# Feed-forward pipeline in another order: the next x is turned in the transposition banks, the row is scaled and clipped by halves between the gate products

## The reference, cut to what matters

```python
def act_quant(x):                       # per token
    scale = 128 / clip(max(abs(x), axis=-1), 1e-5)
    return clip(round(x * scale), -128, 127) / scale
def bitlinear(x, w):   return einsum('bsh,oh->bso', act_quant(x), weight_quant(w))
def h_bitlinear(x, w): return einsum('bsh,oh->bso', act_quant(fwht(x)), weight_quant(w))
gate = bitlinear(x, w_gate)             # 512 -> 2048
up = bitlinear(x, w_up)                 # 512 -> 2048
return h_bitlinear(silu(gate) * up, w_down)   # Hadamard transform of 2048, 2048 -> 512
```

## Time and profile before

| | us |
|---|---|
| median of 3 runs | 2934.85 |
| lowest, highest | 2922.32, 2937.47 |
| the profiled execution | 2938.83 |
| its span in the trace | 2937.1 |
| TensorE products busy | 2063.3 (70%) |
| VectorE busy | 1879.4 (64%) |
| ScalarE busy | 1172.5 (40%) |
| GpSimd busy | 781.1 (27%) |

### The profile page before, as it was taken

How to read it: one execution, slowest core, us unless ns; L and a number is a source line. 1 busy time by engine, 2 the same in 40 slices (tenths; PEclk the granted TensorE clock), 3 DMA queues, 4 the chain that set the end, 5 groups by cost and what they waited for, 6 DMA issues and landing times. The chain is left out here.

```text
span 2937.1 us, 34386 instructions
## 1 busy us (share of the span) xinstructions
PE 2063.3 (70%) x12308; PEld 1395.3 (48%) x12308; DVE 1879.4 (64%) x3042; ACT 1172.5 (40%) x2024; POOL 781.1 (27%) x616
## 2 busy tenths in 40 slices
PE   5999994667777837877749999973002778777760
PEld 5777773222222214444437777751001667555550
DVE  3555664567777746877844566556887343688876
ACT  2323321475655623444422332224882212455640
POOL 1112122015958111111011112220000040466654
PEclk8999997598999869999978999987555589999995
DMA  4333232562524020000032332310000200699965
GB/s 136 95 66 66 45 65 80 147 179 82 153 76 135 18 90 1 1 1 1 1 93 58 66 66 44 66 23 16 0 0 0 103 1 0 234 309 305 307 224 165
DMA packets 83672, 258.06 MB, mean 88 GB/s; under 512 B 17312, under 2 KB 18848, under 8 KB 73424
## 3 DMA queue, kind: packets, MB, share of 16 engines
q0 software_dynamic: 29856, 153.33, 17.4%
q1 hardware_dynamic: 52656, 102.62, 12.7%
q10 hardware_dynamic: 1024, 0.26, 0.0%
HBM read 167.51 MB, written 37.79 MB: 70 GB/s over the span
## 5 line engine op out<-in xcount | busy, mean ns | idle before, releaser
L875 DVE TENSOR_REDUCE x_negm<-x_M 128x2 f32<-128x1024 f32 x256 | 309.3, 1223 | 115.2 <-PE x_M L935 114.8
L824 ACT ACTIVATE x_PT<-x_T 128x512 f32<-128x512 f32 x512 | 280.0, 598 | 202.7 <-PE x_T L955 197.8
L317 ACT ACTIVATE L_attn_PT<-L_attn_T 128x512 f32<-128x512 f32 x320 | 175.5, 595 | 361.1 <-PE L_attn_T L519 361.1
L387 DVE TENSOR_REDUCE L_attn_negm<-L_attn_M 128x2 f32<-128x1024 f32 (+1 forms) x192 | 191.9, 1040 | 58.1 <-PE L_attn_M L500 57.7
L224 POOL DMA_DIRECT2D L_attn_QKS<-L_attn_HL x64 | 34.8, 544 | 597.5 <-ACT L_attn_HL L302 563.7
L955 PE MATMUL x_T<-x_QS,x_KS 49*128 49x512 f32 x512 | 141.2, 548 | 65.6 <-ACT x_PT L824 43.9
L517 PE MATMUL L_attn_T<-L_attn_QKS 97*128 97x256 f32 (+3 forms) x512 | 165.7, 385 | 11.1 <-DMA L_attn_QKS<-L_attn_mT 9.0
L1381 PE MATMUL graph_P<-ident,graph_L 128*128 128x128 f32 x64 | 15.7, 427 | 214.3 <-DVE graph_L L1454 209.0
L964 PE MATMUL x_O<-x_PT,x_V 128*32 128x512 f32 x1024 | 155.7, 684 | 8.2 <-issue 8.2
L1402 ACT ACTIVATE graph_seen_a<-graph_SIM,graph_mid 128x512 bf16<-128x512 f32 x200 | 141.4, 709 | 34.5 <-DVE graph_mid L1434 34.5
L955 PEld LDWEIGHTS x_T<-x_QS,x_KS 49*128 49x128 f32 x512 | 52.1, 200 | 215.8 <-ACT x_PT L824 134.2
(11 more groups left out here) (370 smaller groups left out, 5642.7 us busy)
## 6 DMA issues: line engine op xcount, KB each, us to landing
L_attn_QKS<-L_attn_HL SPq DMA_DIRECT2D x192, 128.0 KB, 4.7
L_attn_QKS<-L_attn_HL POOLq DMA_DIRECT2D x192, 128.0 KB, 4.1
moe_y_rows<-slots_YS SPq DMA_DIRECT2D x48, 256.0 KB, 7.5
x_WRAW<-in_w_gateT POOLq DMA_DIRECT2D x8, 1024.0 KB, 7.3
x_QS<-x_xh SPq DMA_DIRECT2D x128, 64.0 KB, 2.4
x_WRAW<-in_w_upT POOLq DMA_DIRECT2D x8, 1024.0 KB, 5.4
x_WRAW<-in_w_downT POOLq DMA_DIRECT2D x8, 1024.0 KB, 6.2
ffn_w<-x_WTER POOLq DMA_DIRECT2D x12, 512.0 KB, 3.3
```

Source lines behind the costliest of these rows:

```text
L317: ac.activation(PT[:, s, bank], T[:, bank], ACT.Exp, scale=SCALE).then_inc(t_free, 1)
L387: last = ve.tensor_reduce(negm[:, g % 2, h0:h0 + nh, i], src, AX.X, ALU.max, negate=True)
L824: ac.activation(PT[:, s // 4, head(s), :], T[(STEPS_S * g + s) % 3][:], ACT.Exp, scale=SCALE).then_inc(t_free, 1)
L875: ve.tensor_reduce(negm[:, g % 2, u // 4:4:2, u % 4], m[:].rearrange("p (r k) -> p r k", r=2), AX.X, ALU.max, negate=True).then_inc(m_free, 1)
```

## The change

The same instructions are issued in another order, and two buffers change place or size. The next x is turned in the first bank of TT instead of the up bank of GU, between the projection and the second half of the transform, and XQT has two buffers. VectorE copies it behind X. The row's scale (ScalarE) and clip (VectorE) go to the next step, by halves, ahead of silu and INT of its first two quarters. The copies of R are split in the same way, and one butterfly stands ahead of the second split, three behind the second INT. The maximum of the row and its small instructions go behind X and the copy of XQT. The second of the 1024-wide operations goes behind the third INT. The turn of the first half of a row waits for the first two quarters of its tile only, and for the copy of the x that was turned in TT.

```diff
-        XQT = sb("XQT", [P, KC, P], BF16)
+        XQT = sb("XQT", [P, 2, KC, P], BF16)
...
+            def scale(t, v):
+                act.wait_ge(quant, QSTEPS * (t + 1))
+                ac.activation(Y[:, HALVES[v]], Y[:, HALVES[v]], ACT.Identity, scale=yscale[:, 0:1],
+                              bias=magic[:, 0:1]).then_inc(rounded, 1)
...
+            def clip(t, v):
+                if v == 0:
+                    dve.wait_ge(yt_full, 2 * t)
+                dve.wait_ge(rounded, 2 * t + v + 1)
+                ve.tensor_scalar(YQ[:, HALVES[v]], Y[:, HALVES[v]], MAGIC, QB - 1, ALU.subtract, ALU.min).then_inc(yq_done, 1)
...
                 if quantised(s):
                     dve.wait_ge(xt_full, s + 2)
-                    ve.tensor_copy(XQT[:].rearrange("p k n -> p (k n)"),
-                                   GU[:, BANK:BANK + 256].bitcast(BF16)).then_inc(xqt_made, 1)
+                    ve.tensor_copy(XQT[:, (s + 1) % 2].rearrange("p k n -> p (k n)"),
+                                   TT[:, 0:256].bitcast(BF16)).then_inc(xqt_made, 1)
...
             def turn_half(t, v):
                 if v == 0:
-                    if t >= 3:
+                    eng.wait_ge(xqt_made, min(t + 2, NTILE))
+                    if t + 1 >= NTILE:
                         eng.wait_ge(yt_free, 2 * (t - 2))
+                    eng.wait_ge(gu_free, 4 * t + 2)
+                else:
                     eng.wait_ge(gu_free, 4 * t + 4)
-                else:
                     eng.wait_ge(th_free, 2 * t + 1)
...
             def turn_x(t):
-                eng.wait_ge(gu_free, 4 * t)
+                if t >= 4:
+                    eng.wait_ge(yt_free, 2 * (t - 3))
+                elif t >= 2:
+                    eng.wait_ge(th_free, 2 * (t - 1))
                 eng.wait_ge(xq_done, t + 1)
```

More of the change, by code:

```diff
@@ L1136, in gate_up, with butterfly @@
                                         in1=SG[:, u % 2, :], op0=ALU.mult, op1=ALU.mult).then_inc(gu_free, 1)
[L1138 to L1145, removed]
+            def butterfly(t, n):
+                i, j = n // 2, n % 2
+                dve.wait_ge(h_copied, 2 * t + i + 1)
+                inst = ve.tensor_tensor(Y4[:, BANK * n:BANK * (n + 1)], R[i][:, 0:BANK], S13[:, BANK * i:BANK * (i + 1)],
+                                        (ALU.add, ALU.subtract)[j])
+                if n == 3:
+                    inst.then_inc(bf_done, 1)
+            def clip(t, v):
[3 more added lines that the diff above has]
+                ve.tensor_scalar(YQ[:, HALVES[v]], Y[:, HALVES[v]], MAGIC, QB - 1, ALU.subtract, ALU.min).then_inc(yq_done, 1)
             def step(s):
@@ L1151, in step @@
                     lower(s - 1, 0)
+                if projected(s):
+                    clip(s - 3, 0)
                 if gated(s):
@@ L1154, in step @@
                 if scaled(s):
-                    butterfly(s - 2)
+                    butterfly(s - 2, 0)
                 if transformed(s):
                     lower(s - 1, 1)
+                if projected(s):
+                    clip(s - 3, 1)
                 if gated(s):
@@ L1160, in step @@
                 if scaled(s):
+                    for n in range(1, 4):
+                        butterfly(s - 2, n)
+                    dve.wait_ge(bf_done, s - 1)
                     q(ve.tensor_tensor(Y2[:, 0:1024], Y4[:, 0:1024], Y4[:, 1024:], ALU.add))
-                    q(ve.tensor_tensor(Y2[:, 1024:], Y4[:, 0:1024], Y4[:, 1024:], ALU.subtract))
                 if gated(s):
@@ L1170, in step @@
                     q(ve.tensor_tensor(pairs(Y, 1), pairs(Y2, 0), pairs(Y2, 1), ALU.subtract))
+                if projected(s):
+                    t = s - 3
+                    dve.wait_ge(d_full, t + 1)
+                    ve.scalar_tensor_tensor(out=XF[:, t, :], in0=GU[:, 0:BANK], scalar=deq[:, t:t + 1],
+                                            in1=XF[:, t, :], op0=ALU.mult, op1=ALU.add).then_inc(d_free, 1)
+                if quantised(s):
+                    dve.wait_ge(xt_full, s + 2)
+                    ve.tensor_copy(XQT[:, (s + 1) % 2].rearrange("p k n -> p (k n)"),
+                                   TT[:, 0:256].bitcast(BF16)).then_inc(xqt_made, 1)
+                if scaled(s):
+                    t = s - 2
                     q(ve.tensor_reduce(ymax[:], Y, AX.X, ALU.max, apply_absolute_value=True))
@@ L1236, in gate_up @@
                     for k in range(KC):
-                        last = pe.matmul(GU[:, BANK * w:BANK * (w + 1)], XQT[:, k, :], W[:, k, BANK * u:BANK * (u + 1)],
+                        last = pe.matmul(GU[:, BANK * w:BANK * (w + 1)], XQT[:, t % 2, k, :], W[:, k, BANK * u:BANK * (u + 1)],
                                          start=(k == 0), stop=(k == KC - 1))
```

46 lines of the change are left out of this document (17 added, 29 removed).

## The result

| | us |
|---|---|
| changed kernel, median of 4 runs | 2897.34 (2893.98 to 2905.51) |
| before, median of 4 runs | 2936.16 (2922.32 to 2938.59) |
| ratio of the runs | 0.9869, 95% interval 0.9844 to 0.9894 |
| the profiled execution after | 2895.50, span 2893.8 |

What follows compares the result with a forecast made beforehand. A ring of exposed hand-offs between TensorE, ScalarE and VectorE bounds the feed-forward step. Gains 38.9 + 5.4 + 4.8 + 1, less 3 in the drain, make 47.1 us; forecast 2889 us, range 2873 to 2912.

Steps and rivals of the forecast that it cites:

- The ring: Feed-forward step's closed chain of hand-offs between TensorE, ScalarE and VectorE: 19.75 us a step, against 22.84 before.
- The arms beside it: Work parallel to the hand-off chain in a feed-forward step: each fits with 0 to 0.4 us of slack.
- The small waits: VectorE's steady step: pieces of 0.1 to 0.4 us ahead of INT0, INT1, the second split and X.
- step 3: Third feed-forward step: gains 5.4 us from 25.14, or 2 less if the clock stays low.
- the drain: Feed-forward stage's end after INT3 of step 15, 41.2 us before: a loss of 3 us (0 to 5).
- INT3 to INT0: From VectorE's instruction consuming the fourth gate product to the next step's first: 3.47 us instead of 5.00.
- INT1 to INT3: From VectorE's second gate-product instruction to its fourth, through transforms, projection and turn of x: terms adding to 12.81 us.
- The clock rival: Steady feed-forward steps: one fall of TensorE's clock in each, 13 x 1.4 = 18 us less gain, 2907 to 2914; chance 0.06.
- The near-tied arms: Feed-forward step: work parallel to the hand-offs late by 0.4 us at two places, 20.5 a step, 2900; chance 0.17.
- VectorE's floor: Feed-forward step: hand-offs shrink and VectorE's own 18.5 us bound it, 16 us more gain, 2873; chance 0.06.
- No effect: Feed-forward step: the projection wait moves ahead of the row maximum and eats the gain, 2935; chance 0.05.
- slower: Feed-forward step: TensorE stays at 1.2 GHz; at half of the steps 36 us slower, 2971; chance 0.04.

Runs made afterwards that it cites:

- rest_alone: Changed kernel with the turn of x put back in the up bank behind G3, one XQT buffer; step 21.16 us, ratio to the kernel before 0.9913.
- late_quarters: drain_max_first with two of the second transform's four groups moved into the pauses around the next step's G0; step 19.53 us, ratio to the kernel before 0.9839.
- late_again: late_quarters run a second time, beside the changed kernel on the same chip; step 19.53 us, ratio to the kernel before 0.9852.
- max_before_x: Changed kernel with the row maximum and its small instructions back ahead of X; step 21.90 us, ratio to the kernel before 0.9924.
- drain_max_first: Changed kernel with the row maximum ahead of X only in steps without gate products; drain 42.2 us, ratio to the kernel before 0.9853.
- stats_twice: Changed kernel with the statistics of x taken a second time behind INT3 on VectorE (0.60 us more); step 20.07 us, one run.
- pool_sub: late_quarters with the 1024-wide subtraction moved from VectorE to GpSimd; step 20.02 us, ratio to the kernel before 0.9876.

## Why the prediction was right

**The ring.** All seven terms came out within 0.2 us, the sum 1.3% off. The arms beside it stood close to where they were put. INT1 to X is 8.38, against 8.2 for VectorE's work and 8.25 for the end of the projection. The waits for silus are 0.24 to 0.51, forecast as 0.1 to 0.4. The small waits that were forecast ahead of the second split and of X are not marked in the timeline. The stage gained 41.4 us where 47.1 were forecast; the 5.7 are 2.5 in the steady steps, 1.5 in step 3, 1.0 in the drain and 0.7 in steps 1 and 2.

**What was too small.** The steady step is 20.00 and not 19.75. 0.07 of that is in INT3 to INT0: G0 starts 0.90 behind INT3 (1248.88 to 1249.78), where G3 started 0.81 behind X. The rest is in INT1 to INT3, 12.99 in the step shown, where the prediction's terms add to 12.81. The turn of x, 0.27 instead of 0.23, is 0.04 of it. The other 0.13 is in the rest of TensorE's row: rest_alone, without a turn there, takes 12.71 where the terms add to 12.58. I have no experiment for it, nor for the 0.07. The twelve steps average 19.96, since the last has no turn, which makes the 2.5 us in that row of the table.

**Steps 2 and 3.** The forecast of step 3 had 2 us aside for the clock. They were needed. The window of that step, and a steady one for comparison:

```profile
1127.70:1148.90 21.20, 19.39 (x114) 11.94 (x116) 17.69 (x23) 8.92 (x11) 2.61 (x2) 0.92 0.00 1
1208.90:1228.90 20.00, 17.83 (x115) 11.07 (x116) 18.33 (x25) 9.74 (x12) 2.61 (x2) 1.00 0.00 1
```

```profile
1128.58 1.45 PE L1253 MATMUL ffn_GU<-ffn_WG,ffn_XQT 128*128 128x512 bf16 x4 [2.80 <-DVE ffn_INT L1141]
1129.83 1.91 PE L1253 MATMUL ffn_GU<-ffn_WU,ffn_XQT 128*128 128x512 bf16 x4
```

Step 2 has no projection, TensorE has nothing for 2.80 us ahead of G0 of step 3, and its products then ran at the lower level, 1.2 GHz (1.91 for four, and 1.02 in the steady step shown above). So the pause that the forecast thought gone was only halved (5.59 us before). The fall is not the same in every run: with the same program and the same pause, step 3 took 21.14 in late_quarters (pause 2.54, clock 0.92) and 19.56 in late_again (pause 2.55, clock 1.00).

**The clock in the steady part.** It stayed at 1.00 in all twelve steps after step 3, with pauses of 0.84 us and less. The clock rival, one fall in each step, did not come. The prediction's case against it was even stronger than it said: the steady step of the kernel before has a pause of 1.75 us, not only the 1.57 that it named.

```profile
1263.01 1.07 PE L1261 MATMUL ffn_TT<-identb,ffn_YQ 128*128 128x128 bf16 x16 [1.75 <-DVE ffn_ITL L1128]
```

max_before_x pauses 2.02 us in each step, and eleven of its twelve steady steps took 21.9; the twelfth took 22.90, with the granted clock at 0.94. The Trainium skill's rule on clock swings when groups of products go round PSUM banks (TensorE: Matmul & The Clock Gate, A second HAM failure mode: psum-queue depth-cycling) has no support in this trace: 20.00 us a step and not the 21.1 that the prediction made of it. The price of a fall was read too low: it was taken as 1.4 us from TensorE's busy time, but the step with the fall was 1.7 longer than its neighbours.

**The drain.** -4.0 against -3, with the mechanism named: 3.09 us of wait for the projection in step 16. drain_max_first takes 3.0 of the 4.0 back; the cause of the last 1.0 stays open.

**The rivals.** The near-tied arms would have given 20.5; stats_twice shows that one of them takes 0.5 us before it shows. VectorE's floor of 18.5 was not reached by any kernel; 19.53 is the lowest step measured. No effect and slower did not come: X has no marked wait in the steady step, and max_before_x puts the projection's hold on it at 0.1 us, where the first of them needed 3.1. A slip in the sums: 1.8 x 13 on top of 2889 makes 2912, not the 2914 of the clock rival.

## What to carry to other kernels

Where three engines pass one buffer round, write the hand-offs as one ring and sum it; then look for independent work that stands in a queue in front of or behind it and lay it beside the longest wait. What is on the ring costs its full length (0.6 us of 0.62), what stands beside it nearly nothing until the slack is used up (0.1 of 0.60), and a short instruction whose result is waited for in the middle of a queue costs the wait that it puts in front of everything behind it (a turn of 0.4 us, a wait of 1.30, 0.9 us a step). An order that is right for the full pipeline can be wrong in its drain, where the work that covered a wait is missing.

## What the runs showed of the hardware

In pool_sub GpSimd and VectorE slowed each other in two places. GpSimd's 1024-wide subtraction took 3.40 us, beginning beside an addition of two SBUF inputs on VectorE, and 2.4 in the expert stage, where its output has another type. The addition itself was not longer (1.23), and the 1.0 us more is near its length. GpSimd's next instruction took 1.76 beside VectorE's next two additions, the second of which took 1.52; in late_quarters it took 0.69, beside the row maximum, which has one SBUF input. The Trainium skill (SBUF — State Buffer, Who interferes with whom) says that a VectorE instruction with two SBUF inputs contends with a GpSimd instruction that reads SBUF; the trace agrees, though no run here takes the addition away alone.

A turn of four 128-wide blocks costs TensorE 0.23 us of its row ahead of other transposes, and 0.25 to 0.27 between a bf16 projection and an fp32 transform. The start of the transform's first product moves by 0.38, its last by 0.27.
